# Short-key attention on one Trainium2 core: six probability buffers, a pair turned with a lag of two pairs, other products between the two turnings

## Time and profile before

| what | value |
|---|---|
| timed runs, median of 3 | 2700.83 us (2697.91 to 2701.14) |
| profiled execution | 2691.73 us, span 2690.0 us |
| busy PE, PEld | 2387.8 us (89%), 1429.1 us (53%) |
| busy DVE, ACT, POOL | 1607.9 us (60%), 1295.0 us (48%), 1305.6 us (49%) |
| mean granted clock of TensorE | 0.956 |

### The profile page before, as it was taken

How to read it: one execution, slowest core, us unless ns; L and a number is a source line. 1 busy time by engine, 2 the same in 40 slices (tenths; PEclk the granted TensorE clock), 3 DMA queues, 4 the chain that set the end, 5 groups by cost and what they waited for, 6 DMA issues and landing times. The chain is left out here.

```text
span 2690.0 us, 43277 instructions
## 1 busy us (share of the span) xinstructions
PE 2387.8 (89%) x13283; PEld 1429.1 (53%) x13299; DVE 1607.9 (60%) x3274; ACT 1295.0 (48%) x2567; POOL 1305.6 (49%) x2112
## 2 busy tenths in 40 slices
PE   6886999999996996899999999788769985999997
PEld 3554666766663563345444453455546673666664
DVE  5785564755554985777868776587766644212121
ACT  4664343534443794566656667456653431222221
POOL 3665664134445662233443535356775314656663
PEclk9998999999998998999999999899989986999999
DMA  4000000000000005131231311010004151323222
GB/s 138 6 1 32 36 0 0 1 1 1 21 27 16 1 1 126 31 86 41 66 83 37 102 46 48 24 32 17 1 1 165 48 198 25 47 44 47 43 47 28
DMA packets 86180, 115.31 MB, mean 43 GB/s; under 512 B 15624, under 2 KB 65584, under 8 KB 84320
## 3 DMA queue, kind: packets, MB, share of 16 engines
q1 hardware_dynamic: 67456, 92.55, 11.6%
q0 software_dynamic: 18528, 20.31, 4.8%
HBM read 77.92 MB, written 34.64 MB: 42 GB/s over the span
## 5 line engine op out<-in xcount | busy, mean ns | idle before, releaser
L3510 ACT ACTIVATE L2S_pT<-L2S_t_ps 128x512 f32<-128x512 f32 (+3 forms) x768 | 356.4, 491 | 220.9 <-PE L2S_t_ps L3331 212.1
L3574 DVE TENSOR_REDUCE L2S_mx<-L2S_s_ps 128x1 f32<-128x768 f32 (+7 forms) x384 | 350.4, 951 | 106.2 <-PE L2S_s_ps L3254 105.5
L3331 PE MATMUL L2S_t_ps<-L2S_q,L2S_k 98*128 98x512 bf16 (+3 forms) x768 | 249.1, 335 | 18.1 <-DMA L2S_q<-L2S_mrow 7.3
L3816 POOL TENSOR_SCALAR_AFFINE_SELECT L2S_pT<-L2S_pT 128x128 f32<-128x128 f32 x512 | 151.3, 310 | 175.3 <-ACT L2S_pT L3510 171.1
L3253 PE MATMUL L2S_s_ps<-L2S_k,L2S_q 96*128 96x512 bf16 (+3 forms) x768 | 199.5, 332 | 12.1 <-DVE L2S_mx L3574 8.1
L622 POOL TENSOR_TENSOR L_prob<-L_prob,L_rc 128x616 f32<-128x616 f32 x64 | 82.3, 1286 | 231.4 <-DVE L_rc L555 231.4
L4192 DVE TENSOR_TENSOR L3B_h<-L3B_si,L3B_u_ps 128x512 f32<-128x512 f32 x71 | 48.9, 688 | 236.8 <-PE L3B_u_ps L4135 236.8
L4109 POOL DMA_INDIRECT out<-L3B_y,L3F_rows x71 | 114.7, 1616 | 134.5 <-DVE L3B_y L4198 122.2
L3331 PEld LDWEIGHTS L2S_t_ps<-L2S_q,L2S_k 98*128 98x128 bf16 x768 | 73.0, 98 | 196.8 <-ACT L2S_pT L3510 127.6
L3431 PE MATMUL L2S_o_ps<-L2S_pT,L2S_v 128*32 128x512 f32 (+3 forms) x1536 | 165.6, 504 | 0.0
L319 PE MATMUL L_scores<-weights,L_xT 128*128 128x308 f32 x512 | 143.1, 423 | 2.2 <-ACT L_xT L442 1.6
(11 more groups left out here) (549 smaller groups left out, 5723.9 us busy)
## 6 DMA issues: line engine op xcount, KB each, us to landing
qk_parts<-L2S_part SPq DMA_DIRECT2D x84, 128.0 KB, 2.4
L2S_q<-qk_parts SPq DMA_DIRECT2D x32, 192.0 KB, 3.4
L2S_k<-qk_parts SPq DMA_DIRECT2D x30, 192.0 KB, 3.4
L2S_q<-qk_parts SPq DMA_DIRECT2D x32, 128.0 KB, 3.1
L3F_w<-in_L_gu SPq DMA_DIRECT2D x8, 512.0 KB, 7.3
weights<-in_L_w SPq DMA_DIRECT2D x8, 512.0 KB, 9.4
out<-x_sb SPq DMA_DIRECT2D x8, 512.0 KB, 3.6
expert_rows<-L_xn SPq DMA_DIRECT2D x8, 512.0 KB, 2.9
```

Of the source, the lines that this page charges most:

```text
L3331: nc.tensor.matmul(o[:, lo:512], k6[:, q % 2, j, kt * P:(kt + 1) * P], q6[:, q % 2, c, j, lo:512], start=True, stop=True).then_inc(s["t_fu ...
L3510: nc.scalar.activation(pT[:, st % SLOTS, j, lo:512], t_ps[j % 2][:, lo:512], ACT.Exp, scale=SK).then_inc(s["exp_done"], 1)
L3574: nc.vector.tensor_reduce(dst, src, AX.X, ALU.max).then_inc(s["mx_done"], 1)
L3816: nc.gpsimd.affine_select(out=edge, in_=edge, compare_op=ALU.is_ge, fill=0.0, base=0, pattern=[[1, P]], channel_multiplier=-1).then_inc(s[ ...
```

## The change

In both stages the `prob` buffers (and the small `sm` and `rc`) become six (`HELD`), and the pair of step s-4 is turned in step s (`BEHIND`). `STEPS` of the first stage grows by 2. The products get other places in `ring_uses`, and a new function `pieces` says what goes ahead of the first turning (gathers), between the two turnings, and after the second one. In a step with a gather everything else of the step, that of odd u too, goes between the turnings.

```diff
-    STEPS = UNITS + UN + 2
+    STEPS = UNITS + UN + 4
+    HELD, BEHIND = 6, 4
-        prob, probT = sb("prob", [P, PBUF, HK]), ...
+        prob, probT = sb("prob", [P, HELD, HK]), ...
...
         def ring_uses(g, u):      # first stage
-            if u == 1 and 2 <= g <= G + 1:
-                uses += [("c", g - 2, 3)]
+            if g + 1 < G and u == 0:
+                uses += [("x", g + 1, dh) for dh in range(KD)]
+            if 2 <= g <= G + 1:
+                uses += {1: [("c", g - 2, 1), ("c", g - 2, 2)], 2: [("c", g - 2, 3)]}.get(u, [])
             if g + 1 < G:
-                uses += {0: [("x", g + 1, dh) for dh in range(KD)], 1: [("q", g + 1, 0)], 3: [("q", g + 1, 1)]}.get(u, [])
+                uses += {3: [("q", g + 1, 0)], 5: [("q", g + 1, 1)]}.get(u, [])
             if 1 <= g <= G:
-                uses += {2: [("o", g - 1, 0)], 4: [("o", g - 1, 1)], 5: [("c", g - 1, 0)], 6: [("c", g - 1, 1)], 7: [("c", g - 1, 2)]}.get(u, [])
+                uses += {4: [("o", g - 1, 0)], 6: [("o", g - 1, 1)], 7: [("c", g - 1, 0)]}.get(u, [])
             if u == 7 and g % 2 == 0 and g // 2 + 1 < B:
                 uses += [("v", g // 2 + 1)]
...
         def ring_uses(g, u):      # second stage
             if 1 <= g <= G:
-                uses += {2: [("o", g - 1, 0)], 4: [("o", g - 1, 1)], 5: [("c", g - 1, 0)], 6: [("c", g - 1, 1)]}.get(u, [])
+                uses += {4: [("o", g - 1, 0)], 6: [("o", g - 1, 1)], 7: [("c", g - 1, 0)]}.get(u, [])
+            if u == 0 and 2 <= g <= G + 1:
+                uses += [("c", g - 2, 1)]
...
+        def pieces(s):            # both stages
+            g, u = divmod(s, UN)
+            even, odd = ring_uses(g, u), ring_uses(g, u + 1)
+            ahead = [use for use in even if use[0] == "o"]
+            rest = even[len(ahead):]
+            return (ahead, rest + odd, []) if ahead else ([], rest, odd)
...
             for s in range(0, STEPS, 2):      # PE, both stages
+                ahead, middle, late = pieces(s)
                 if s < UNITS:
                     scores(s)
+                for use in ahead: ...
+                if 0 <= s - BEHIND < UNITS:
+                    turn(s - BEHIND)
+                for use in middle: ...
+                if 0 <= s - BEHIND < UNITS:
+                    turn(s - BEHIND + 1)
+                for use in late: ...
...
             for s in range(0, STEPS, 2):      # ACT, both stages
+                if ahead:    # exp(s), ahead, turn(s - BEHIND)
+                else:        # turn(s - BEHIND), middle[:1], exp(s)
+                for use in middle if ahead else middle[1:]: ...
+                    turn(s - BEHIND + 1)
                 if s < UNITS:
                     exp(s + 1)
+                for use in late: ...
...
             def unit(U):          # DVE
-                if U >= PBUF:
-                    dve.wait_ge(t_full, U - PBUF + 1)
+                if U >= HELD:
+                    dve.wait_ge(t_full, U - HELD + 1)
```

More of the change, by code:

```diff
@@ L842, in _ @@
             for s in range(0, STEPS, 2):
-                g, u = divmod(s, UN)
-                first = ring_uses(g, u)
+                ahead, middle, late = pieces(s)
                 if s < UNITS:
                     scores(s)
[L847 to L857, removed]
+                for use in ahead:
+                    piece[use[0]](*use[1:])
+                if 0 <= s - BEHIND < UNITS:
+                    turn(s - BEHIND)
+                for use in middle:
+                    piece[use[0]](*use[1:])
+                if 0 <= s - BEHIND < UNITS:
+                    turn(s - BEHIND + 1)
+                for use in late:
                     piece[use[0]](*use[1:])
@@ L938, in _ @@
                         exp(s)
[L939 to L942, removed]
+                for use in middle if ahead else middle[1:]:
+                    piece[use[0]](*use[1:])
+                if 0 <= s - BEHIND < UNITS:
+                    turn(s - BEHIND + 1)
                 if s < UNITS:
                     exp(s + 1)
-                for use in ring_uses(g, u + 1):
+                for use in late:
                     piece[use[0]](*use[1:])
@@ L1168, in ring_uses, with pieces @@
             return uses
+        def pieces(s):
+            g, u = divmod(s, UN)
+            even, odd = ring_uses(g, u), ring_uses(g, u + 1)
+            ahead = [use for use in even if use[0] == "o"]
+            rest = even[len(ahead):]
+            return (ahead, rest + odd, []) if ahead else ([], rest, odd)
         def ring_fills():
@@ L1352, in _ @@
             for s in range(0, LAST, 2):
-                g, u = divmod(s, UN)
-                first = ring_uses(g, u)
-                ahead = [use for use in first if use[0] == "o"]
+                ahead, middle, late = pieces(s)
                 if s < UNITS:
@@ L1359, in _ @@
                     piece[use[0]](*use[1:])
-                if 0 <= s - 2 < UNITS:
-                    turn(s - 2)
-                for use in first[len(ahead):]:
+                if 0 <= s - BEHIND < UNITS:
+                    turn(s - BEHIND)
+                for use in middle:
                     piece[use[0]](*use[1:])
-                if 0 <= s - 2 < UNITS:
-                    turn(s - 1)
-                for use in ring_uses(g, u + 1):
+                if 0 <= s - BEHIND < UNITS:
+                    turn(s - BEHIND + 1)
+                for use in late:
                     piece[use[0]](*use[1:])
@@ L1463, in _ @@
                         piece[use[0]](*use[1:])
-                    if 0 <= s - 2 < UNITS:
-                        turn(s - 2)
-                else:
-                    if 0 <= s - 2 < UNITS:
-                        turn(s - 2)
-                    for use in first[:1]:
+                    if 0 <= s - BEHIND < UNITS:
+                        turn(s - BEHIND)
+                else:
+                    if 0 <= s - BEHIND < UNITS:
+                        turn(s - BEHIND)
+                    for use in middle[:1]:
                         piece[use[0]](*use[1:])
@@ L1472, in _ @@
                         exp(s)
-                for use in first[max(1, len(ahead)):]:
+                for use in middle if ahead else middle[1:]:
                     piece[use[0]](*use[1:])
-                if 0 <= s - 2 < UNITS:
-                    turn(s - 1)
+                if 0 <= s - BEHIND < UNITS:
+                    turn(s - BEHIND + 1)
                 if s < UNITS:
                     exp(s + 1)
-                for use in ring_uses(g, u + 1):
+                for use in late:
                     piece[use[0]](*use[1:])
```

60 lines of the change are left out of this document (30 added, 30 removed).

## The result

The changed kernel took 2680.99 us (median of 6 runs, 2674.28 to 2687.72) against 2699.27 us for the kernel before in the same sitting (6 runs, 2692.85 to 2701.14): a ratio of 0.9936, 95% interval 0.9917 to 0.9956, a gain of 17 to 18 us where 15.6 were forecast. The profiled execution took 2679.3 us for a span of 2677.5 us, with a mean granted clock of 0.955 (before: 0.956).

The account below looks back on a forecast made before the run. Neither TensorE nor VectorE is full, so who waits for whom bounds the kernel. Gains of 2.5+4.1-0.4 (first stage) and 7.7+0.7+1.0 (second), 15.6 us, taken from the 2700.83 median give 2685.2; 8-in-10 range 2664 to 2702.

Parts of the forecast that it names:

- (a): Both stages, six buffers and lag of two pairs: buffers only pay for the lag; turnings' waits for POOL's division become zero.
- rival A: Both stages: the whole wait for the division, 15.8 and 19.1 us, was on the path, giving 2665.9 us; chance 0.12.
- (b): First stage, step 2 loses its gather to steps 4 and 6: 4.87 us for 7.45, a gain of 2.6.
- (c): First stage, step 4 with the query between its two turnings: 7.13 us for 6.77, a loss of 0.4.
- (d): First stage, step 6: combine 0 waits for the gather's eviction; 7.05 us for 4.87, loss 2.2; 9.2 with values.
- (e): First stage, step 0 stays at VectorE's 6.76 us, with combines 1 and 2 after the second turning.
- what I gave as its reason: First stage, group 0: query no longer ahead of second scores, no turning waits for a fresh division; gain 4.1 us.
- B: Nothing is left: steps 4 and 6 eat the gains, exponential 0.5 us later per step; 2699 us, chance 0.18.
- C: Slower: new TensorE idle in steps 4 and 6 drops its clock, losing 23.8 us; 2709 us, chance 0.14.
- the two that I named: Second stage before the change, low-clock stretches: 0.66 over five microseconds from 1860, another in group 5; 1.7 us lost.

Follow-up runs that it names:

- E3: Changed kernel with the lag back at one pair, six buffers and the new places kept: 2719.09 us, ratio 1.0084 to the kernel before.
- E2: Changed kernel with four buffers and a lag of one pair, new places kept: 2718.64 us, ratio 1.0079 to the kernel before.
- E6: Changed kernel with products back at their old places as far as the lag allows, first gather one half-step later: 2676.33 us, ratio 0.9932 to the kernel before.
- E4: Changed kernel with ScalarE's second exponential ahead of evictions between turnings and second copy, in steps with a gather: 2663.20 us, ratio 0.9880 to the kernel before.
- E7: E4 with combine 0 of the first stage moved to the next group's step 0: 2659.52 us, ratio 0.9867 to the kernel before.
- E5: E2 with POOL's first-stage updates moved behind the division: 2695.94 us, ratio 1.0001 to the kernel before.
- E10: E6's kernel unchanged, run again for a second profile: 2680.44 us.
- E8: The changed kernel unchanged, run again for a second profile: 2681.59 us.

## Why the prediction was right, and where not

The time and the sign were right (2685.2 forecast), and most steps stood where they were put. That the total came so near is partly luck: by the first profiles the first stage gave 9.2 us for 6.3 forecast and the second 7.8 for 9.4, and the two misses partly cancel.

(a) That the buffers give nothing by themselves: shown by E3 against E2. That the lag sets the waits for the division to zero: it does for the matmuls (0.9 us and none left); the 7.8 and 6.6 us that stayed are weight loads'. I had read those rows as the turnings' own wait; rival A's 34.9 us are 19.7 in the matmuls (6.9 and 12.8). The mis-sized term is here: I gave the lag a price only in group 0 (4.1) and none in the steady groups, since I took group 3's step 0 of 6.76 us for all of them, and let the order of the products decide there. In groups 2, 4 and 6 it was 7.07, with the turning's 0.71 us in it. The square says the reverse: in the first stage all the gain is that of the lag and of the gather's move that it forces.

(b), (c), (d) held to 0.2 us: forecast 4.87, 7.13, 7.05, measured 4.88, 6.94, 6.96 in group 3; 9.2 with values, measured 9.15. Their sum is near nothing, as worked out, and E6 shows it from the other side: with the lag, old and new places make the same group (25.39 and 25.47), and with values the old ones the shorter (26.94 and 27.65). (d) named the right wait, but E4 shows that its cost passes through ScalarE's order; E7 that taking TensorE's wait away after that gives 0.26 us in a step, 1.6 with values.

(e) held: step 0 at 6.69.

The first stage's groups 1 to 7 gained 5.3 us (178.24 to 172.94), not 2.5: each of groups 1 to 5 came out 0.3 shorter than forecast, and group 6 1.1, since its step 0 has no statistics (5.35 us); I had counted that for group 7 alone. Group 0 gained 4.24 where 4.1 was forecast, but 1.2 of it is not what I gave as its reason: step 0 took 7.95 us before because its query ran at half clock (3.62 us for 1.98, 0.66 granted from 35 to 40 us, in both profiles of that kernel). E6's second profile, with the query in its old place at 1.00, has 6.74 there. The end lost 0.15 for 0.4.

The second stage's groups 1 to 7 gained 6.35 us (211.43 to 205.08), not 7.7. Groups 2 to 7 were within 0.6 us of the forecast each and 1.7 better together; group 1 took 32.27 where I had 29.2. I had not carried the price of values in step 6 into it: that step took 10.49 us, like the other steps with values (10.58 and 10.13), and 6.18 before. The stage's group 0 gave 0.25 for 0.7, its end after the last step 6 1.2 for 1.0.

The rivals. A (2665.9): out, step 6 is at 6.96, and E6, which takes the waits away with the old places, reached 2676.33 and not 2665.9. B (2699): out for this kernel; its time is what came of the places without the lag (E5, 2695.94). C: its case was the second stage, and I had counted the low stretches there short. Besides the two that I named, 0.68 was granted from 1805 to 1810 us, where step 0 of group 3 took 8.95 us for 7.63 in group 5, and 0.66 from 1950 to 1955. Groups 1 to 7 of the second stage, before and after (busy us and instructions of PE, PEld, DVE, ACT, POOL; granted clock):

```profile
1751.94:1963.37 211.43, 174.52 (x1342) 114.05 (x1341) 164.62 (x327) 128.87 (x227) 141.00 (x172) 0.95 0.05 16
...
1745.97:1951.05 205.08, 170.16 (x1311) 107.91 (x1315) 166.46 (x327) 127.94 (x225) 140.91 (x171) 0.95 0.05 16
```

The new waits did not lower the clock there: it is 0.95 in both, and the low stretches have only moved (0.66 from 1794 to 1799 and from 1824 to 1829 us after the change). In the first stage it held in the steady groups (0.99 over the loop). It fell in group 0 in some executions of the variants, of the kernel before and of the changed kernel; in the last its steps 0 and 2 are no longer for it (6.74 and 4.87 us, as in E6's second profile at 1.00). The window of the first loop, in the same columns, answers to the earlier trace rows:

```profile
32.00:228.00 196.00, 168.66 (x1410) 104.77 (x1406) 166.58 (x306) 126.14 (x212) 120.25 (x136) 0.99 0.02 6
```

VectorE's busy share rose from 164.68 of 205 (80%) to 166.58 of 196 (85%).

What stays open: whether the gather behind step 2's turnings would give its 3.9 us without the lag; why the new places lengthen the first stage's end; and what lets the clock fall in one execution and not in the next.

## What to carry to other kernels

When a software-pipelined loop runs on queues written in order, a longer lag and a new order are two changes: try each alone, since here the lag, with the one move that it forces, gave the whole gain and the rest of the new order only moved time from one stage to the other. When a product is moved, move what every other engine does for it as well: updates left at their old place on POOL cost 21 to 23 us (E2 against E5, by the ratios and by the medians), and an exponential left behind evictions on ScalarE 15 to 18 us (the changed kernel against E4). Of several waits in a step, the one that sets it is the one whose removal moves the next step's first instruction; the table of waits does not say which. In that table tell a wait of the weight loads (PEld) from one of the matmuls (PE).

## What the runs showed of the hardware

One kernel gets another clock of TensorE in the same instructions from one execution to the next. Group 0 of the first stage, five microseconds at a time (busy us and instructions of PE, PEld, DVE, ACT, POOL; then the granted clock), first in E6:

```profile
35.00:40.00 5.00, 4.55 (x20) 1.94 (x24) 4.13 (x13) 1.80 (x3) 1.79 (x2) 0.66 0.01 3
...
50.00:55.00 5.00, 4.12 (x28) 3.41 (x22) 4.68 (x8) 2.44 (x5) 2.42 (x3) 0.50 0.19 61
```

then in E10, the same kernel:

```profile
35.00:40.00 5.00, 4.82 (x28) 2.02 (x26) 4.75 (x15) 1.33 (x2) 2.51 (x3) 1.00 0.02 3
...
45.00:50.00 5.00, 3.00 (x33) 2.03 (x32) 4.86 (x9) 3.66 (x6) 2.14 (x2) 1.00 0.22 65
50.00:55.00 5.00, 5.00 (x55) 4.49 (x54) 4.60 (x9) 3.63 (x6) 2.52 (x3) 1.00 0.00 0
```

0.50 is the lower level, 1.00 the upper. TensorE's work before the fall in E6 and at the same place in E10, as matmul rows with the idle time before them:

```profile
46.73 0.74 PE L824 MATMUL L_turned<-ident,L_prob 128*128 128x128 f32 x5 [0.89 <-ACT L_probT L902]
48.58 0.72 PE L811 MATMUL L_scores<-L_maskb,L_identb 128*128 128x308 bf16 x4 [1.11 <-DVE L_prob L1001]
49.23 1.41 PE L815 MATMUL L_scores<-L_kblk,L_qT 32*128 32x154 f32 x16
```

```profile
44.66 0.74 PE L824 MATMUL L_turned<-ident,L_prob 128*128 128x128 f32 x5 [0.89 <-ACT L_probT L902]
46.51 0.72 PE L811 MATMUL L_scores<-L_maskb,L_identb 128*128 128x308 bf16 x4 [1.11 <-DVE L_prob L1001]
47.16 0.81 PE L815 MATMUL L_scores<-L_kblk,L_qT 32*128 32x154 f32 x16
```

The idle times are the same, 0.89 and 1.11 us; the score products that follow take 1.41 us in the one and 0.81 in the other, and the group 26.08 and 22.10. So these idle times alone do not decide the clock. But the two executions had differed before that, 0.66 against 1.00 from 35 to 40 us, and what decides it is not shown. In E8 the low stretch came earlier (0.56 over 35 to 40 us) and cost nothing: VectorE was busy 4.79 of those 5.00 us, and steps 0 and 2 took 6.74 and 4.87 us, as long as in E10 at 1.00. The Trainium skill's page "TensorE: Matmul & The Clock Gate" (Part 1) says that the throttled state is the default and that activity releases it, and that one kernel has more or fewer throttled matmuls at its start from run to run; here the low stretch lies within the loop, and the trace agrees in that it varies between the runs of one kernel.
